# A patch of one-hot additions and a second output column moved from VectorE and ScalarE to GpSimd, and three nibble entries instead of four

## The reference

```python
x = x + conv(_ln_c(x))          # 3x3 box filter, each channel alone, weights 1/9, zero padding
t = _to_tokens(x)               # one token per pixel, 256 features (the channels)
t = t + ffn(_ln_t(t))           # _ln: (v - mean) / sqrt(var + eps) over the channels
```

```python
x_ge = zeros(..., 8, 80)                       # position 0 and 1 are used
x_ge[..., 0, 0] = nibble(x, 16)                # nibble(x, b) = argmax(x[..., b:b+16] > 0.5)
x_ge[..., 1, 0] = nibble(x, 32)
x_ge[..., 0, 1] = nibble(x, 48)
x_ge[..., 1, 1] = nibble(x, 32)                # the same sixteen columns as above
x_ge[..., :, 35] = x[..., 65];  x_ge[..., :, 36] = x[..., 66]
mark = x[..., 0] > 0.5
m_add = mark & (x[..., 1] > 0.5)
m_sub = mark & ~(x[..., 1] > 0.5) & (x[..., 2] > 0.5)
y = where(m_add, mlp(x_ge, Wa, ba), where(m_sub, mlp(x_ge, Ws, bs), x_ge))    # three 80x80 layers, ReLU between
out[..., 64:80] += 2 * one_hot(clip(round(y[..., 0, 50]), 0, 15)) * active
out[..., 72:88] += 2 * one_hot(clip(round(y[..., 1, 50]), 0, 15)) * active
out[..., 80]    += (round(y[..., 1, 79]) > 0.5) * active
```

## Time and profile before

| what | value |
|---|---|
| median of the runs | 617.44 us |
| the profiled execution's own time | 618.25 us |
| its span, first to last instruction | 616.5 us |
| TensorE (PE) busy | 479.6 us, 78% |
| VectorE (DVE) busy | 507.8 us, 82% |
| ScalarE (ACT) busy | 468.7 us, 76% |
| GpSimd (POOL) busy | 383.9 us, 62% |
| mean granted TensorE clock | 0.961 of full |
| DMA queue q1, share of 16 engines | 88.5% |

### The profile page before, as it was taken

One profiled execution on the slowest core, in us unless ns is written; L12 is line 12 of the kernel. 1 busy time (PEld: TensorE's weight loads), 2 busy tenths in 40 slices (PEclk: granted clock), 3 DMA queues, 4 the chain that ended last, 5 costly groups with the idle time before them and its releaser, 6 DMA issues.

```text
span 616.5 us, 8862 instructions
## 1 busy us (share of the span) xinstructions
PE 479.6 (78%) x2294; PEld 201.1 (33%) x2294; DVE 507.8 (82%) x1476; ACT 468.7 (76%) x675; POOL 383.9 (62%) x676
## 2 busy tenths in 40 slices
PE   0035369999989988988899999988999999997750
PEld 0012123333333434333333333433333333433220
DVE  1378979999999999999999999999999999874130
ACT  0011569888888888899999888888888888998730
POOL 0044767777777777777777777777777777764000
PEclk9997779999999999999999999999999999998885
DMA  9999990099877995699559958960598099898998
GB/s 168 191 193 199 193 164 2 0 109 170 133 104 104 171 172 68 103 166 190 80 78 176 173 89 110 137 70 1 68 115 92 1 103 69 64 75 62 88 87 72
DMA packets 592746, 67.97 MB, mean 110 GB/s; under 512 B 592568, under 2 KB 592696, under 8 KB 592696
## 3 DMA queue, kind: packets, MB, share of 16 engines
q1 hardware_dynamic: 591696, 67.30, 88.5%
q10 hardware_dynamic: 1000, 0.11, 0.1%
HBM read 33.84 MB, written 33.55 MB: 109 GB/s over the span
## 4 chain that ended last, share of the span: by engine, by line
DVE 33%; PE 32%; POOL 12%; ACT 11%; issue 5%; SPq 3%; DMA 1%; DVEq 0%; POOLq 0%; ACTq 0%
PE ps L864 13%; PE ps L895 10%; POOL nlo L650 10%; DVE n L542 9%; DVE stat L552 7%; ACT nhi L816 5%; PE ps L918 4%; DVE g L505 4%; DVE xbuf L570 3%; ACT xbuf L771 3%; SPq L287 3%; PE ps L887 2%; DVE ps L481 2%; ACT h L791 1%; PE ps L900 1%
## 5 line engine op out<-in xcount | busy, mean ns | idle before, releaser
L771 ACT ACTIVATE xbuf<-xbuf,shift,gain 128x256 f32<-128x256 f32 x224 | 200.4, 944 | 0.0
L552 DVE BATCH_NORM_STATS2 stat<-xbuf 128x6 f32<-128x512 f32 x256 | 171.2, 685 | 22.0 <-DMA xbuf<-x 21.8
L650 POOL TENSOR_TENSOR nlo<-n,nhi 128x1024 f16<-128x1024 f32 x64 | 137.5, 2149 | 7.5 <-ACT nhi L816 7.4
L895 PE MATMUL ps<-h,w2m 128*128 128x512 f32 x256 | 134.3, 607 | 3.7 <-ACT h L791 2.4
L864 PE MATMUL ps<-nhi,band 128*128 128x512 f16 (+1 forms) x408 | 108.4, 380 | 25.1 <-POOL nlo L650 25.1
L669 POOL TENSOR_SCALAR n<-xbuf,stat,rns 128x256 f32<-128x256 f32 x64 | 94.2, 1478 | 41.4 <-DVE ps L456 41.0
L542 DVE SCALAR_TENSOR_TENSOR n<-xbuf,stat,ps 128x256 f32<-128x256 f32 x192 | 118.8, 663 | 0.1
L864 PE MATMUL ps<-nlo,band 128*128 128x512 f16 (+1 forms) x408 | 107.4, 377 | 0.0
L570 DVE TENSOR_TENSOR xbuf<-ps,xbuf 128x512 f32<-128x512 f32 x128 | 91.5, 715 | 15.6 <-PE ps L864 15.5
L816 ACT ACTIVATE nhi<-n 128x1024 f16<-128x1024 f32 x64 | 67.5, 1054 | 46.6 <-DVE n L542 46.6
L791 ACT ACTIVATE h<-ps,b2m 128x512 f32<-128x512 f32 x128 | 88.0, 687 | 11.4 <-PE ps L895 11.3
(11 more groups left out here) (90 smaller groups left out, 560.0 us busy)
## 6 DMA issues: line engine op xcount, KB each, us to landing
xbuf<-x SPq DMA_DIRECT2D x32, 512.0 KB, 6.9
xbuf<-x SPq DMA_DIRECT2D x16, 1024.0 KB, 11.1
out<-xbuf SPq DMA_DIRECT2D x32, 512.0 KB, 7.4
out<-xbuf SPq DMA_DIRECT2D x12, 1024.0 KB, 12.6
out<-xbuf SPq DMA_DIRECT2D x16, 256.0 KB, 8.3
consts<-cst SPq DMA_DIRECT2D x1, 176.0 KB, 2.4
h<-ws ACTq DMA_DIRECT2D x4, 0.2 KB
b2r<-bs ACTq DMA_DIRECT2D x4, 0.1 KB
```

What stands on the lines that cost most here:

```text
L552: return v.bn_stats(stat[:, j % 4, at + 2 * s:at + 2 * s + 2, :].rearrange("p w n -> p (w n)"), xview(par)[:, w:w + 2, :].rearrange("p w c ...
L650: pool.tensor_tensor(nlo[:, at:at + HALF, :], n32[:, h, :, :], nhi[:, at:at + HALF, :], ALU.subtract).then_inc(lo_ready, 1)
L771: ins = act.activation(col, col, ACT.Identity, bias=shift[:, k, w:w + 1], scale=gain[:, k, w:w + 1])
L895: pe.matmul(ps[:, B_L2, :], w2m[:, :], h1[:, slot(i, jc), :], start=True, stop=True).then_inc(l2_done, 1)
```

## The change

GpSimd writes columns 6 and 7 of a chunk's output (before: 7 alone), behind the features instead of ahead of the masks; ScalarE writes six. The additions of one-hot rows and carry leave VectorE; GpSimd does them at the end of its step, in four instructions chained by the new semaphore `hot_p`: the one-hot values times two, an addition for each of the two ranges, and the carry. `hot` and `ycar2` move from PSUM to SBUF for that, and `put(0)` on VectorE waits until GpSimd has finished those of the chunk before. The high nibble stands in the value vector once, with the sum of its two weights, so `NV` is 10 and one small GpSimd product goes; the two first masks are made by one instruction instead of two.

```diff
-NV = 11
-V_LO, V_HI, V_ONE = 6, 8, 10
+NV = 10
+V_NIB, V_ONE = 6, 9
...
+OUT_P = 6
...
-        subraw = sb("subraw", [P, CW], F32)
+        hot = sb("hot", [P, CW, 2, NIB], F32)
+        ycar2 = sb("ycar2", [P, CW], F32)
...
-                    sp.wait_ge(hotc, chunks_by(pair, h) * HOT_STEPS)
+                    sp.wait_ge(hot_p, chunks_by(pair, h) * HOT_P)
...
-                    for at in (V_LO, V_HI):
-                        v.tensor_copy(base[:, k, at:at + 2], nat[:, k, 0:2])
+                    v.tensor_copy(base[:, k, V_NIB:V_NIB + 3:2], nat[:, k, 0:2])
+                    v.tensor_tensor(base[:, k, V_NIB + 1:V_NIB + 2], nat[:, k, 0:1], nat[:, k, 1:2], ALU.add)
...
             def result(i, last, k):
...
                     v.wait_ge(yt_done, c + 1)
+                    wait(v, hot_p, HOT_P * c)
...
-                elif i in (5, 6):
-                    at = OUT_LO if i == 5 else OUT_HI
-                    v.wait_ge(out_ready, c + 1)
-                    v.wait_ge(out_p, c + 1)
-                    hc.count(v.scalar_tensor_tensor(cols[:, :, at:at + NIB], hot[:, :, i - 5, :], 2.0,
-                                                    cols[:, :, at:at + NIB], ALU.mult, ALU.add))
-                else:
-                    hc.count(v.tensor_tensor(cols[:, :, CARRY], cols[:, :, CARRY], ycar2, ALU.add))
                     hc.end()
...
-                put(5)
...
-                put(6)
...
-                put(7)
...
+            hp = Chain(pool, hot_p, HOT_P)
...
-                    w, k = CW - 1, (j - 1) % 4
-                    col = xview(par)[:, jc * CW + w, :]
-                    pool.tensor_scalar(col, col, gain[:, k, w:w + 1], shift[:, k, w:w + 1], ALU.mult,
-                                       ALU.add).then_inc(out_p, 1)
...
-                    pool.tensor_tensor(msk[:, k4, :, 0], marks[:, b2i, :, 0], marks[:, b2i, :, 1], ALU.mult)
-                    pool.tensor_tensor(subraw[:, :], marks[:, b2i, :, 0], marks[:, b2i, :, 2], ALU.mult)
+                    pool.tensor_tensor(msk[:, k4, :, :], over(marks[:, b2i, :, 0:1], [P, CW, 2]),
+                                       marks[:, b2i, :, 1:3], ALU.mult)
...
-                    pool.tensor_tensor(val[:, :, V_LO:V_LO + 2], nfree[:, :, 0:3:2], nhit[:, :, 0:3:2], ALU.mult)
-                    dc.count(pool.tensor_tensor(val[:, :, V_HI:V_HI + 2],
-                                               over(nfree[:, :, 1:2], [P, CW, 2]),
-                                               over(nhit[:, :, 1:2], [P, CW, 2]), ALU.mult))
+                    dc.count(pool.tensor_tensor(val[:, :, V_NIB:V_NIB + 3], nfree[:, :, :], nhit[:, :, :], ALU.mult))
...
                     ins.then_inc(feat_ready, 1)
                     dc.end()
-                    pool.wait_ge(feat_ready, c + 1)
+                    k = (j - 1) % 4
+                    for w in range(OUT_P, CW):
+                        col = xview(par)[:, jc * CW + w, :]
+                        ins = pool.tensor_scalar(col, col, gain[:, k, w:w + 1], shift[:, k, w:w + 1], ALU.mult,
+                                                 ALU.add)
+                    ins.then_inc(out_p, 1)
+                if last:
+                    c, jc, par = last
+                    cols = xview(par)[:, jc * CW:(jc + 1) * CW, :]
+                    hp.turn(c)
+                    pool.wait_ge(out_ready, c + 1)
+                    pool.wait_ge(out_p, c + 1)
+                    pool.wait_ge(hotc, HOT_STEPS * (c + 1))
+                    hp.count(pool.tensor_scalar(hot[:, :, :, :], hot[:, :, :, :], 2.0, None, ALU.mult))
+                    hp.wait()
+                    for i, at in enumerate((OUT_LO, OUT_HI)):
+                        hp.count(pool.tensor_tensor(cols[:, :, at:at + NIB], cols[:, :, at:at + NIB],
+                                                    hot[:, :, i, :], ALU.add))
+                        hp.wait()
+                    hp.count(pool.tensor_tensor(cols[:, :, CARRY], cols[:, :, CARRY], ycar2[:, :], ALU.add))
+                    hp.end()
+                if tok:
+                    pool.wait_ge(feat_ready, tok[0] + 1)
...
-HOT_STEPS = 8
+HOT_STEPS = 5
+HOT_P = 4
```

More of the change, by code:

```diff
@@ L218, in build @@
         eps, r_0, r_n = (own(2 * CW) for _ in range(3))
-        thalf, rn, thr, ycar2 = (own(CW) for _ in range(4))
+        thalf, rn, thr = (own(CW) for _ in range(3))
         yr = own(4 * CW).rearrange("p (b m o) -> p b m o", b=CW, m=2)
         yrr, ycar = (own(2 * CW).rearrange("p (b m) -> p b m", m=2) for _ in range(2))
-        hot = own(2 * CW * NIB).rearrange("p (b m n) -> p b m n", b=CW, m=2)
         rank = own(3 * NIB)
@@ L261, in build @@
         hotc = sem("hotc")
+        hot_p = sem("hot_p")
         def xview(parity):
@@ L401, in setup_parts @@
                 done(ins)
-                for pos, at in ((0, V_HI), (1, V_LO)):
+                for pos, at in ((0, V_NIB + 1), (1, V_NIB), (1, V_NIB + 2)):
                     rows = tl[:, pos, 0:ROWS].rearrange("p (r v) -> p r v", v=NV)
-                    ins = v.memset(rows[:, :, at:at + 2], 0.0)
+                    ins = v.memset(rows[:, :, at:at + 1], 0.0)
                 done(ins)
@@ L458, in result @@
             def result(i, last, k):
-                c, jc, par = last
-                cols = xview(par)[:, jc * CW:(jc + 1) * CW, :]
+                c = last[0]
                 if i == 0:
@@ L473, in result @@
                 if i == 1:
-                    v.tensor_reduce(ycar2, ycar, mybir.AxisListType.X, ALU.add).then_inc(y_read, 1)
+                    v.tensor_reduce(ycar2[:, :], ycar, mybir.AxisListType.X, ALU.add).then_inc(y_read, 1)
                     hc.count(v.tensor_scalar(yr, yr, 1.0, float(NIB), ALU.max, ALU.min))
@@ L643, in step @@
                 tok = chunk_at(t, j, pair, 3)
+                last = chunk_at(t, j, pair, 6)
                 k4 = (j - 3) % 4
@@ L707, in step @@
                     dc.wait()
-                    pool.tensor_tensor(msk[:, k4, :, 1], subraw[:, :], noadd[:, :], ALU.mult)
-                    pool.tensor_tensor(val[:, :, V_LO:V_LO + 2], nfree[:, :, 0:3:2], nhit[:, :, 0:3:2], ALU.mult)
-                    dc.count(pool.tensor_tensor(val[:, :, V_HI:V_HI + 2],
-                                               over(nfree[:, :, 1:2], [P, CW, 2]),
-                                               over(nhit[:, :, 1:2], [P, CW, 2]), ALU.mult))
+                    pool.tensor_tensor(msk[:, k4, :, 1], msk[:, k4, :, 1], noadd[:, :], ALU.mult)
+                    dc.count(pool.tensor_tensor(val[:, :, V_NIB:V_NIB + 3], nfree[:, :, :], nhit[:, :, :], ALU.mult))
                 if norm:
@@ L715, in step @@
                 if tok:
-                    c = tok[0]
+                    c, jc, par = tok
                     dc.wait()
@@ L772, in columns @@
                                              scale=gain[:, k, w:w + 1])
-                    if end == CW - 1:
+                    if end == OUT_P:
                         ins.then_inc(out_ready, 1)
@@ L802, in step @@
                     if s == 0 and ffn:
-                        columns(ffn, (j - 2) % 4, OUT_AT[GROUPS - 1], CW - 1)
+                        columns(ffn, (j - 2) % 4, OUT_AT[GROUPS - 1], OUT_P)
                     if s == 0 and ffn:
```

6 lines of the change are left out of this document (3 added, 3 removed).

## The result

The changed kernel takes 711.35 us (median of 4 runs, 710.46 to 712.06), the kernel before 617.7 us in the same comparison (a fourth run, 618.1, beside the three already shown): a ratio of 1.1519, 95% interval 1.1496 to 1.1543. Slower, by 94 us. The forecast was 704, with a range of 682 to 740.

The account below looks back on a forecast made before the run. The prediction took a circle closed by put(0)'s wait for GpSimd's whole step as the bound: 90 - 4 - 1 + 1.5 = +86 us on 618.25, forecast 704 us, range 682 to 740.

Parts of the forecast that it names:

- The bound before: Circle from VectorE's put(0) through GpSimd's low half to TensorE's last convolution work and the next put(0): 16.15 us a step.
- the new circle: put(0) waits for GpSimd's whole step, which starts 3.96 us after put(0): the step is GpSimd's busy stretch plus 3.96 us.
- The size of the step: Steps 6 to 32: 19.48 us instead of 16.15, 3.33 more, 27 times, 90 us.
- GpSimd's start to the end of the features: GpSimd's work ahead of its columns, with the features done 1.24 us earlier than before, at 319.23.
- two columns: GpSimd's output columns behind the features: 0.90 us each, 1.74 in all after small overlaps.
- doubling: GpSimd's one-hot values times two, 256 elements: 0.95 us, with ends of 0.45 and 1.48.
- each addition: GpSimd's two additions of 128 elements to the output: 0.50 us each, with ends of 0.44 and 0.8.
- carry and three waits: End of GpSimd's step: 0.20 us for the carry of 8 elements, and three chain waits of 0.08 each.
- the terms -4 and +1.5: Last steps: TensorE gives back its lead once, -4 us; late channels of the last parts are stored later, +1.5 us.
- The start: First steps: features come over a microsecond earlier, once, -1 us.
- TensorE's clock, the rival: TensorE, idling 4 to 5 us a step, drops to 1.2 GHz and becomes the bound: 736 us, chance 0.08.
- VectorE's and ScalarE's savings: VectorE's 0.92 us a step lies ahead of put(0), where it already waits; ScalarE's column lies beside TensorE: no gain.

Follow-up runs that it names:

- e1: Changed kernel with hot and ycar2 in two buffers by turn, put(0) waiting for the chunk before last: 619.95 us.
- e2: Changed kernel with single hot, two ycar2 buffers, and the wait moved from put(0) to put(4), which writes hot: 651.29 us.
- e3: Changed kernel with OUT_P = 7, so ScalarE writes seven columns and GpSimd one: 682.6 us.
- e11: Changed kernel with GpSimd's two output columns behind the four result instructions instead of ahead of them: 656.54 us.
- e10: Changed kernel with GpSimd doing the result instructions first in steps 33 and later: 704.14 us.
- e4: Kernel before without VectorE's additions of one-hot rows and carry, which are not done at all: 612.3 us.
- e9: Changed kernel with doubled buffers, two statistics instructions ahead of put(0), and GpSimd's result instructions first in steps 33 and later: 596.21 us.

## Why the prediction was right, point by point

**The bound before and the new circle**: right. 28 waits for L734 took the place of TensorE's, 91.6 us where 70 to 100 were named. e1 opens the circle and 91 of 94 us go; e2, e3 and e11 take 2.3, 1.04 and 1.99 us out of it by three different cuts, and 27 times that is 62, 28 and 54 us of the 60, 29 and 55 that were measured.

**The size of the step**: 19.48 forecast, 19.64 measured, of which 27 steps make 94 us instead of 90. Within it, measured as means over the steps 6 to 32:

| term | forecast | measured |
|---|---|---|
| `put(0)` to GpSimd's start | 3.96 | 3.96 |
| GpSimd's start to the end of the features | 11.26 | 11.20 |
| two columns | 1.74 | 1.92 (1.79 to 2.02) |
| doubling | 0.95 | 0.89 |
| each addition | 0.50 | 0.53 |
| carry and three waits | 0.44 | 0.45 |
| `hot_p` to VectorE | 0.13 | 0.15 |

The one term mis-sized by more than 0.1 us is that of the columns. I took L697's 0.90 for each, and the mean was 1.064; the last section says when they are slower. Doubling and additions were between the ends, and their errors, -0.06 and twice +0.03, cancel. That the doubling came so near is in part luck. The slope of 3 ns an element came from one row of 24 elements (L706, 0.275); the row of the same size beside it (L705, 0.209) gives 0.4 ns by the same working, and so 0.30 us at 256 elements. What held was the other anchor, L697 with 0.90. By the Trainium skill's cycles for a tight loop (GPSIMD Engine Reference, section 3.1) the doubling was estimated at 0.58 us; the trace has 0.884, and the measurement decides.

**The end**: the terms -4 and +1.5 were wrong in kind, and their sum by 3 us. I let TensorE's lead be given back in steps 33 to 35 and the last stores be late by the last chunks' additions. From `put(0)` of step 33 to the end it took 616.5 - 545.94 = 70.6 before and 710.2 - 638.99 = 71.2 now. TensorE did give back its lead (`put(0)` of step 35 came 26.1 us after that of step 33, 29.3 before), but the end hangs on the result of chunk 27 in step 33, with 57.7 us of stores behind it. e10 shows it: with that result early the empty stretch of the queue is gone, and with it 7 us. That result was in place 12.7 us after its `put(0)` before and 13.5 now, which is the term as measured: +0.7 where I had -2.5. **The start**: -1, measured -0.97 (108.84 for 109.81).

Sum: 94.0 - 1.0 + 0.7 = 93.7, the two spans differ by 93.7. The forecast's 86 lacks 4 us of the steps and 3 us of the end.

**TensorE's clock, the rival**: its mechanism came in 21 of the 27 steps, and stayed hidden. TensorE in the changed kernel, after its idle stretch in a step:

```profile
354.70 1.44 PE L872 MATMUL ps<-nhi,band 128*128 128x512 f16 x3 [4.33 <-POOL nlo L643]
355.94 1.48 PE L872 MATMUL ps<-nlo,band 128*128 128x512 f16 x3
357.22 0.44 PE L895 MATMUL ps<-featT,w 128*128 128x512 bf16 x1
357.50 1.02 PE L903 MATMUL ps<-h,w2m 128*128 128x512 f32 x2
358.36 0.81 PE L872 MATMUL ps<-nhi,band 128*128 128x512 f16 x3
```

The first convolution group runs at the 1.2 GHz level, as the earlier trace rows, the second at 2.4 again. The busy time by stretch of the same step (PE, PEld, DVE, ACT, POOL, PEclk, DMA, GB/s) shows the granted clock beside it:

```profile
348.70:352.50 3.80, 1.68 (x10) 0.30 (x2) 3.80 (x8) 1.29 (x2) 3.55 (x6) 1.00 1.12 142
352.50:354.80 2.30, 0.10 (x1) 0.13 (x2) 2.30 (x5) 2.30 (x4) 2.30 (x3) 0.81 0.13 24
354.80:358.00 3.20, 3.20 (x9) 1.25 (x9) 1.93 (x4) 3.04 (x5) 2.91 (x9) 0.60 1.25 197
358.00:361.00 3.00, 3.00 (x15) 1.46 (x13) 2.70 (x6) 2.74 (x5) 3.00 (x4) 1.00 0.79 124
```

The mean over the span fell from 0.961 to 0.908. It costs TensorE some 1.3 us in such a step and the kernel nothing: from step 7 to 33 L926 ended 1.1 to 3.6 us before `put(0)` started, in most steps over 2. By the Trainium skill (TensorE: Matmul & The Clock Gate, part 1) activity lifts the throttle, and with that rule the trace agrees. I expected the loss in every step, and in six it did not come. In e1 the circle is open and the clock of steps 6 to 33 is 1.00 throughout.

**VectorE's and ScalarE's savings**: right for the changed kernel, as e4's steady part shows, but e4's 612.3 lies under the 614 that I gave, because the additions stand late in a step and the last stores wait for them: without them the result of chunk 27 is complete at 548.4 us instead of 558.7.

## What to carry to other kernels

Idle time of an engine is room for work only if nobody ahead of that engine waits for the end of the added work: follow the new wait around once, and add up the whole round. If the round is longer than the old one, a second buffer can move the wait one turn back; here that was worth 91 us, with no instruction saved. And before crediting work taken off an engine, look for what will be put into the gap: VectorE's 0.92 us a step brought nothing in the steady steps (e4) until two instructions moved into its wait, and then up to 9 us.

## What the runs showed of the hardware that was not expected

GpSimd's column instruction took 0.89 to 0.91 us in 32 of 32 cases before, but 1.064 on average in the changed kernel. e11 has both cases in one run. Its columns without any column of ScalarE at the same time took 0.88 to 0.93 each; those with 0.65 us or more of overlap took 1.04 to 1.28 each. GpSimd of e11 in order of time, first alone, then together with ScalarE:

```profile
337.44 1.77 POOL L735 TENSOR_SCALAR xbuf<-xbuf,gain,shift 128x256 f32<-128x256 f32 x2
...
372.77 2.02 POOL L735 TENSOR_SCALAR xbuf<-xbuf,gain,shift 128x256 f32<-128x256 f32 x2
```

and ScalarE of e11 beside the second of them, at the pixel column just ahead of GpSimd's two:

```profile
372.62 1.30 ACT L780 ACTIVATE xbuf<-xbuf,shift,gain 128x256 f32<-128x256 f32 x1
```

Both get slower, ScalarE's from 0.94 to 1.30. Both step through `xbuf` by 256 bytes. It isn't every overlap. In the changed kernel's step 34 GpSimd's two columns ran beside ScalarE's columns 2 and 3, for 0.7 and 0.9 us and started within 0.3 us of them, and took 0.90 each. Over all thirteen traces the column that ScalarE is at tells the cases apart. Of GpSimd's columns (6 or 7 of a chunk) that overlapped ScalarE's by 0.65 us or more, the 204 beside column 4 or 5 took 1.04 to 1.31 us, and the 7 beside columns 0 to 3 took 0.89 to 0.93. So a common start is not enough, and the address counts. The distance alone is not it either: with some 0.5 us of overlap, column 7 beside column 4 took 0.98 to 1.01, and column 6 beside column 3, three columns away as well, took 0.91 (one case, in e9). Columns 4 to 7 of a chunk lie within 16 bytes in each channel, and column 3 lies outside them. That these 16 bytes decide is a guess from the pattern, which no run tried.

The Trainium skill (SBUF — State Buffer, "SBUF: two separate sides") says that on the engine side only the port pair shared by VectorE and GpSimd causes contention and that ScalarE never waits; these rows differ from it, and the measurement decides.

The end of the kernel is limited by stores of 16 pixel columns, 64 bytes a piece. From the queue's last empty stretch to the end they moved 85 to 87 GB/s on average in each of the thirteen traces, and 71 to 95 in single stretches of 6 us, whatever the engines did.
